# First graph layer: mask added to the logits per edge, linear part of the leaky logits from the product, node sums in two halves

## The reference

```
h = relu(layernorm(x));  x = x + L0(h);  h = relu(layernorm(x));  x = x + L1(h)
L0: msg   = project(h)[src] + project(h)[dst]                # 64 scalars, 32 vectors
    m1    = tensor_product(msg, y, rbf @ W_rbf)              # 96 scalars, 128 vectors
    a     = m1_s @ W_alpha                                   # 4 heads x 16
    a     = sum(leaky_0.2(a) * alpha_dot, over the 16)       # one logit for each edge and head
    alpha = softmax of a over the edges of each dst node
    val   = gates and sigmoids of m1 @ W_val
    h_e   = tensor_product(val, y, w2) @ W_vlin
    out   = h + (sum over the edges of a node of alpha * h_e) @ W_p
```

## Time and profile before

| | |
|---|---|
| median of 3 runs | 10575.95 us (10566.82 to 10586.68) |
| profiled execution: own time, span | 10573.21 us, 10571.2 us |
| busy: PE, DVE, POOL, ACT | 80%, 70%, 59%, 31% of the span |
| mean granted TensorE clock | 0.899 of full speed |

### The profile page before, as it was taken

One profiled execution on the slowest core, in us unless ns is written; L12 is line 12 of the kernel. 1 busy time (PEld: TensorE's weight loads), 2 busy tenths in 40 slices (PEclk: granted clock), 3 DMA queues, 4 the chain that ended last, 5 costly groups with the idle time before them and its releaser, 6 DMA issues. The chain is left out here.

```text
span 10571.2 us, 201187 instructions
## 1 busy us (share of the span) xinstructions
PE 8497.0 (80%) x50848; PEld 6425.6 (61%) x50849; DVE 7420.9 (70%) x18020; ACT 3241.5 (31%) x8443; POOL 6191.2 (59%) x6291
## 2 busy tenths in 40 slices
PE   1388888888888888888888888877658888888888
PEld 1277777777777777777777777766433333333335
DVE  2477777777777777777777777666237777777775
ACT  0133333333333333333333333322222222222223
POOL 0266666666666666666666666543007777677774
PEclk9599999999999999999999999888558888889889
DMA  2133333333333333333333333222002222222221
GB/s 35 48 83 81 83 83 81 82 83 82 81 85 81 84 83 81 83 83 82 83 82 82 83 81 83 71 61 52 8 12 57 57 57 58 58 57 57 57 57 48
DMA packets 560992, 725.68 MB, mean 69 GB/s; under 512 B 228019, under 2 KB 334899, under 8 KB 560956
## 3 DMA queue, kind: packets, MB, share of 16 engines
q0 software_dynamic: 225792, 385.65, 16.3%
q1 hardware_dynamic: 335164, 339.61, 12.1%
HBM read 708.76 MB, written 16.06 MB: 69 GB/s over the span
## 5 line engine op out<-in xcount | busy, mean ns | idle before, releaser
L739 PE MATMUL bank_pair<-w_msg,blocks 128*128 128x160 f32 (+1 forms) x15640 | 2420.7, 318 | 768.1 <-DVE blocks L983 768.1
L739 PEld LDWEIGHTS bank_pair<-w_msg,blocks 128*128 128x128 f32 x15640 | 2314.5, 219 | 859.3 <-DVE blocks L983 859.3
L1377 POOL DMA_INDIRECT gotf<-f_tab,idx x1568 | 1712.8, 1092 | 748.5 <-issue 383.9
L697 POOL DMA_INDIRECT got_src<-src_tab,idx x1568 | 1520.4, 970 | 726.6 <-POOL idx L691 368.3
L697 POOL DMA_INDIRECT got_dst<-dst_tab,idx x1568 | 1495.8, 954 | 529.3 <-issue 527.5
L761 PEld LDWEIGHTS bank_pair<-weights_t,product 128*128 128x128 f32 x12896 | 1493.9, 194 | 309.1 <-issue 294.9
L761 PE MATMUL bank_pair<-weights_t,product 128*128 128x128 f32 x12896 | 1570.5, 281 | 8.9 <-ACT weights_t L885 8.2
L1417 PE MATMUL bank_pair<-val,to_node 128*128 128x449 f32 x3136 | 1477.3, 619 | 6.0 <-DVE val L1520 6.0
L706 POOL TENSOR_TENSOR edge<-rbf,y 128x512 f32<-128x512 f32 x391 | 661.1, 1691 | 1244.5 <-PE bank_pair L728 1137.5
L894 ACT ACTIVATE weights<-near,small 128x512 f32<-128x512 f32 x391 | 282.2, 722 | 3014.1 <-DVE small L933 3014.1
L1468 ACT ACTIVATE val<-pre,y_edge 128x160 f32<-128x160 f32 x1568 | 542.9, 417 | 1894.1 <-DVE pre L1508 1894.1
(11 more groups left out here) (267 smaller groups left out, 12953.8 us busy)
## 6 DMA issues: line engine op xcount, KB each, us to landing
rbf<-in_rbf SPq DMA_DIRECT2D x392, 256.0 KB
dst_bc<-in_dst_rows SPq DMA_DIRECT2D x391, 256.0 KB
y<-in_y SPq DMA_DIRECT2D x392, 128.0 KB
y<-in_y SPq DMA_DIRECT2D x392, 96.0 KB
got_src<-src_tab,idx POOLq DMA_INDIRECT x1568
got_dst<-dst_tab,idx POOLq DMA_INDIRECT x1568
gotf<-f_tab,idx POOLq DMA_INDIRECT x1568
rbf<-in_rbf SPq DMA_DIRECT2D x392, 32.0 KB
```

Of the source, the lines that this page charges most:

```text
L697: pool.indirect_dma_start(out=buf[slot][:, t, :], out_offset=None, in_=table[:, :], in_offset=bass.IndirectOffsetOnAxis(ap=idx[slot][:, c: ...
L739: return nc.tensor.matmul(to, blocks[rows, k, P * t:P * t + P], w_msg[rows, c0:c1], start=start, stop=stop)
L1377: pool.indirect_dma_start(out=got[k % 2][:, t, :], out_offset=None, in_=f_tab[:, :], in_offset=bass.IndirectOffsetOnAxis(ap=idx[k % 2][:, ...
```

## The change

1. The mask moves from the turned logits (128 rows x 512 edges) to the edges (128 edges x 4 tiles x 32 nodes). A table `keys` is made once; per group DVE makes `apart` (is the node not this edge's, 128 x 128) and multiplies it by -1e30 (`bar`), in the middle of the step. `widen` at the end of DVE's tail adds mask and logit into `logits_wide` (128 x 512), which ACT no longer writes. After PE's transpose the turned logits already hold the mask, so DVE takes only the row maximum (`tensor_reduce`), and ACT's exponentials read PSUM. `far`, `near`, `ring`, `dst_bc` and its DMA go.
2. The linear part 0.2*a, summed with `alpha_dot`, comes as 4 more columns of `w_msg` (164 in place of 160 in two pieces of five). DVE's tail becomes relu part times `alpha_dot`, sum over 16 into `bent`, then `logits = columns 160..163 + bent` (128 x 16).
3. PE: two quarters of `sum_products`, `weigh(1)`, the other two quarters, `spread_logits`, `message_tile(0)`, and only then `project`; then `message_tile(1)`, `(2)`, and on as before. In place of the wait for `top`, the next transposes wait for nothing of DVE.
4. ACT copies the projected window out of PSUM (`picked`, four pieces of 32 rows); DVE's `take_window` is one instruction on SBUF and waits for it. PE's next sums wait for `picked` in place of `win_scaled`.
5. DVE: `multiply` is cut in two. Order: blocks 0 and 1, `multiply_vectors` (5 instructions), blocks 2 and 3, `multiply_scalars` (3), `apart`, `bar`, `take_window`, `add_sums`, maximum, peak, tail with `widen`. The two last peak updates become one.
6. `more` windows use the banks of `weigh` in place of the turn banks, and the same mask, maximum and `picked`.

```
 PE     if late:
            pe.wait_ge(s["picked"], g - 2)
            sum_products(slot, 0, 2)
        if now:
            pe.wait_ge(s["block_done"], g * 4 + 2)
            weigh(1, 0); weigh(1, 1)
        if late:
-           sum_copied wait; project(); more
+           sum_products(slot, 2, 4).then_inc(s["window_sum"], 1)
        if mid:
            spread_logits(other, turn_low)
        if now:
            pe.wait_ge(s["block_done"], g * 4 + 4)
-           for t in range(3): message_tile(t)
+           message_tile(0)
+       if late:
+           pe.wait_ge(s["sum_copied"], g - 1)
+           project().then_inc(s["projected"], 1)      # then more
+       if now:
+           for t in range(1, 3): message_tile(t)
        if mid:
            pe.wait_ge(s["weights"], g)
            turn_weights(turn_high)
 ACT
+    def pick():
+        for h in range(HEADS):
+            r = slice(BLK * h, BLK * h + BLK)
+            last = nc.scalar.activation(picked[r, :], win[r, h, :], ACT.Copy)
...
        hold().then_inc(s["sum_copied"], 1)
+       act.wait_ge(s["projected"], g - 1)
+       pick().then_inc(s["picked"], 1)
 DVE
+    def widen(slot, mask):        # [P, TILES, HEADS, BLK]
+        logits_wide[slot] = mask (repeated over heads) + logits[slot] (repeated over nodes)
+    def bar(mask):  mask = mask * least
...
-       multiply(g - 1, other)
-       dve.tensor_scalar(far[:], dst_bc[other][:], ring[:, at_group(g - 1)], LEAST, not_equal, mult)
+       multiply_vectors(g - 1, other)
        messages(g, 2)
+       multiply_scalars(g - 1, other)
+       dve.tensor_tensor(apart[:], iota_row ..., keys_of(g), not_equal)
+       bar(apart)
-       dve.wait_ge(s["projected"], g - 1)
+       dve.wait_ge(s["picked"], g - 1)
        take_window(g - 2); add_sums(b)
-       dve.tensor_tensor_reduce(out=near, in0=turn_low, in1=far, ..., accum_out=top)
+       dve.tensor_reduce(top, turn_low, axis=AX.X, op=max)
...
-       for b2 in range(2): dve.scalar_tensor_tensor(lg[two], a, 0.2, rl[two], mult, add)
-       dve.tensor_tensor(lg[:], lg[:], adot ..., mult)
+       dve.tensor_tensor(lg[:], rl[:], adot ..., mult)
        gated
-       dve.tensor_reduce(logits[:], lg ...)
+       dve.tensor_reduce(bent[:], lg ...)
+       dve.tensor_tensor(logits[slot], scalars[:, :, :, 160:164], bent, ALU.add)
+       widen(slot, apart).then_inc(s["logit_wide"], 1)
```

More of the change, by code:

```diff
@@ L541, in _ @@
                         dve.memset(y8[i][64:96, :], 1.0)
+                    dve.memset(least[:], LEAST)
+                    for i in range(2):
                         dve.memset(product[i][:, :, 0, 96:97], 1.0)
@@ L598, in layer0 @@
         gated = tmp("gated", [P, TILES, D])
-        logits = tmp("logits", [P, TILES * HEADS])
+        logits = [tmp(f"logits{i}", [P, TILES, HEADS]) for i in range(2)]
+        bent = tmp("bent", [P, TILES, HEADS])
+        apart = tmp("apart", [P, TILES, BLK])
+        apart_more = tmp("apart_more", [P, TILES, BLK])
         logits_wide = [tmp(f"logits_wide{i}", [P, TILES, P]) for i in range(2)]
-        far = tmp("far", [P, GE])
-        far_more = tmp("far_more", [P, GE])
-        near = tmp("near0", [P, GE])
         weights = tmp("weights", [P, GE])
@@ L893, in step @@
                             act.wait_ge(s["weights_turned"], g - 1)
-                        nc.scalar.activation(weights[:], near[:], ACT.Exp, bias=minus).then_inc(s["weights"], 1)
+                        nc.scalar.activation(weights[:], turn_low, ACT.Exp, bias=minus).then_inc(s["weights"], 1)
                         act.wait_ge(s["rescale"], g)
@@ L1019, in step @@
                             dve.wait_ge(s["product"], g - 1)
-                        multiply(g - 1, other).then_inc(s["product"], 1)
-                        dve.wait_ge(s[f"dst{other}"], mid_use(slot, use) * 16 + 16)
-                        if late:
-                            dve.wait_ge(s["top"], g - 1)
-                        dve.tensor_scalar(far[:], dst_bc[other][:], ring[:, at_group(g - 1)], LEAST, ALU.not_equal,
-                                          ALU.mult).then_inc(s["far"], 1)
+                        multiply_vectors(g - 1, other)
                     if now:
                         messages(g, 2)
+                    if mid:
+                        multiply_scalars(g - 1, other).then_inc(s["product"], 1)
+                    if now:
+                        dve.tensor_tensor(apart[:], iota_row[:, 0:BLK].unsqueeze(1).broadcast_to([P, TILES, BLK]), keys_of(g),
+                                          ALU.not_equal).then_inc(s["masked"], 1)
+                        dve.wait_ge(s["masked"], g * 2 + 1)
+                        bar(apart).then_inc(s["masked"], 1)
                     if mid or late:
```

226 lines of the change are left out of this document (123 added, 103 removed).

## The result

| | before | after |
|---|---|---|
| median, us | 10575.04 | 10880.26 |
| lowest to highest (4 runs each) | 10566.82 to 10586.68 | 10859.98 to 10904.61 |
| profiled execution: time, span | 10573.21, 10571.2 | 10904.61, 10902.8 |
| period of a group, 1000 to 6500 us | 17.21 | 18.07 |

The changed kernel takes 1.0289 times as long (95% interval 1.0265 to 1.0312). In a later set of runs the same pair gave 1.0295 (1.0275 to 1.0315).

A forecast was written before the change was run, and what follows sets the result against it. No engine was full; a serial DVE-then-PE loop bound it, with PE waiting for the fourth block. 391 x (18.2 - 17.2) = 390, plus 10 setup and 10 windows, on 10573.21 gave about 10,980 us; range 10,740 to 11,200, whole range 10,400 to 11,330.

The forecast's parts named there:

- the fourth block's wait: PE's 2.0 us a group before the messages, standing for DVE's fourth block; claimed gone or under 0.5 us.
- loop at full clock, no hold-up: One serial loop through PE, ACT and DVE from `vec` to the next `vec`: 17.36 us, against 16.7 before.
- half clock: Turn and tile 3 at half rate after PE's 2.4 us stand, two groups in three: 0.8 us, bounds 0 and 1.66.
- The step that did fail: DVE's scalar products, `apart` and `bar` before `take_window`: reached at about 10 us, hidden beside project and pick, costing nothing.
- The rule as the prediction puts it: A DVE instruction with two SBUF inputs and a GpSimd instruction reading SBUF exclude each other for a whole instruction.
- the 1.0 that the prediction read: The wait inside DVE's `far` before the change: 1.0 us of its 1.50, since its shortest is 0.474.
- Rival (d): POOL's `edge` precedes the last vector product in every group, which waits about 1.3 us: period 18.9, time 11,250; chance 0.15.
- Rival (b): Clock term small or pick-to-exponentials chain a bit shorter: period 17.0 to 17.6, time 10,520 to 10,740; chance 0.18.
- Rival (c): Pick, take and maximum hide behind tiles 1 and 2, leaving PE's 15.2 us: 9,810; chance 0.17 with in-between cases.
- The 16.7: Old loop's length in us at full clock, from 3022.82 to 3039.52 in the trace, through DVE and then PE.
- setup: Making `keys` before the groups: eight instructions over 1568 values a row, about 10 us, exposed before POOL's first gather.
- The 10 for the 12 extra windows: The 12 extra windows gain `pick` and `widen`, lose pieces of the same size: 1 us each at most, 10 summed.

The follow-up runs named there:

- PE filled: Changed kernel plus eight unused products on PE where it stands before `turn_weights`: 10659.76 us, 1.0073 of the kernel before; on another chip 13126.58 us, 1.0531.
- project early: Changed kernel with PE's projection before `message_tile(0)` instead of behind it: 12941.55 us, 1.0378 of the kernel before on that chip; repeated 12937.62 us, 1.0366.
- POOL late: POOL's `edge` and `msg` wait for DVE's drops: in the changed kernel 11716.9 us, 0.9396 of the kernel before; in the kernel before 10028.37 us, 0.9475.
- 0.9038: Changed kernel with PE's old order restored and POOL's `edge` and `msg` behind DVE's drops: 11259.28 us on a chip running the kernel before in 12486.33.
- POOL late and project early: Changed kernel with projection before tile 0 and POOL's `edge` and `msg` behind DVE's drops: 10267.16 us, 0.9702 of the kernel before; on another chip 11616.61, 0.9322.

## Why the prediction came out right, and which terms did not

Time 10,880 against 10,980 forecast; period 18.07 against 18.2. The mechanism is the one forecast: the fourth block's wait is gone, `weigh(1)` has a wait of 0.57 in the group shown (1.0 forecast; at most 0.8, and none seen in 88 of 305 groups), and the loop closes through pick, take, maximum and exponentials. One sign did not come: the clock was to be under 0.94 in the steady part, and it was 0.95. And the size comes from two terms that were off by as much, one up and one down; that they cancelled is luck.

| us a group | predicted | measured |
|---|---|---|
| loop at full clock, no hold-up | 17.36 | 16.59 |
| POOL holding off DVE | 0 | 0.78 (17.37 - 16.59) |
| half clock | 0.8 | 0.70 (18.07 - 17.37) |
| period | 18.2 | 18.07 |

The 0.78 is read from the groups with and without a hold-up in PE filled. No run on a chip of 10,575 us took the hold-up alone out of the changed kernel; with project early as well the period was 16.41 at clock 1.00.

The loop, step by step from T0, in the group at 3011.87 (forecast in brackets): blocks 0 and 1 3.13 (3.17), `weigh(1)` 4.46 (4.50), tile 0 7.85 (7.94), project 9.08 (9.24), picks 10.20 (10.47), `take_window` 11.06 (11.41), maximum 12.10 (12.65), exponentials 13.93 (14.50), turn 14.67 (15.27), `vec` 16.59 (17.36). No step of this chain failed; small ones leaned the same way: 0.27 up to the picks, picks 0.83 for 0.9, 0.15 before the maximum for 0.33, turn to `vec` 1.92 for 2.09.

The step that did fail, beside the chain, reads: "They lie beside the project and pick wait, as does the rest of what is taken off DVE; it costs and gains nothing." It put DVE at `take_window` at about 10. DVE is ready for it only at 10.8 to 12.3, for two reasons. First, I had two POOL instructions in the traces and followed one: `edge` starts at 5.81 and takes 1.40, and meets blocks 2 and 3, which keep their 1.28. `msg` behind it meets `product += along` or `bar` and holds one of them for 1.2 to 1.35. Line 1046 takes 1.097 on average (333.43 us in 304 times), so it is hit in some (1.097 - 0.28) / 1.35 = 60% of the groups. Second, the register read: before, it stood behind blocks 2 and 3, 1.28 us of work, and cost nothing; now only `bar`, 0.29, covers it, and 1.0 to 1.1 us is seen.

By the Trainium skill's rule (SBUF — State Buffer, "Who interferes with whom") the trace agrees: the pairs that exclude each other have two SBUF inputs on DVE, the blocks with an input in PSUM run beside `edge` undisturbed, and with POOL late both sides fall to their shortest, 1.55 and 0.28. The rule as the prediction puts it doesn't reach `far`, which has one 128x512 input and was held off too. It lost less than the 1.0 that the prediction read: with POOL late it takes 0.676, not 0.474, so 1.493 - 0.676 = 0.82.

Rival (d) named this mechanism at another place, the last vector product. That one (line 1036) takes 0.29 in the median and up to 1.38; its 98.20 us in 304 times leave room for some ten such groups, so (d) did not happen in every group, but its price did, one step later, where I had given it no chance. Rival (b) was half right: the chain was shorter, by 17.36 - 16.59 = 0.77, more than (b) had. Its time fell with the hold-up, and with the clock: 0.70 a group is 274 us of 391 groups. (The chance of faster, (c) and a fifth of (b), comes to 0.21, not 0.22.) Rival (c) fell with the waits.

The same split of the kernel before: 15.84 without hold-up at clock 1.00, so hold-up and clock together were 17.21 - 15.84 = 1.37. The 16.7 that the prediction took for the old loop at full clock held `far`'s hold-up. In the changed kernel the two are 1.48. What the change adds is thus mostly the loop itself: 0.75 of 0.86 us a group. With POOL late in both kernels, and project early in the changed one, it still costs 0.57: 16.41 against 15.84, 10267 against 10028 us.

The other terms: setup 8.8 to 10.0 for 10. The 10 for the 12 extra windows is not seen: 390 x 0.86 = 335 alone exceeds the loop's 322.9.

Left open: the keys, the widened logits and the product columns were never tried without PE's new order on a chip of 10,575 us, so 0.9038 is not shown to hold there. Why PE filled and project early lie so high on the other chips (1.0531 and 1.0378) is open too. Moving the register read ahead of the wait, the obvious next edit, was not tried, so its price is read from traces alone.

## What to carry to other kernels

Before adding work to a busy engine's cover, ask what another engine does to it there: list every GpSimd instruction that reads SBUF with the DVE instructions that it meets, and move it to where DVE is idle; on the kernel before, that one wait gave 5.3%, more than this change cost. When an edit removes the wait that closes the loop, follow the next chain through all engines to the end, register reads behind a semaphore wait included. A forecast can hit by errors that cancel, so check each term with a kernel that removes it alone.

## What the runs showed of the hardware

- `marks_of` behind a semaphore wait leaves 1.00 to 1.12 us idle ahead of DVE's next instruction when only 0.29 us of work covers it; the load itself takes 0.305, the register operation behind it 0.190, and taking the numbers out of the word makes up most of the rest, 0.045 for each operation.
- The same kernel ran in 10575 and 10576 us in two sets of runs, and in 12475 and 12486 us on two other chips. Traces of kernels on the latter have waits of up to 10.3 us put down to `remote` (POOL late and project early, ACT's `held`), which the former's don't have.
- Hold-up is not symmetric in cost: POOL's 640-column sum went from 1.55 to as much as 3.51 us, DVE's 128-column one from 0.28 to 1.62, and which DVE instruction is hit decides whether it costs anything.
